# A three-layer transformer block on one core: first rows over two queues and two engines, gathers of first and second choices signalled apart, last results stored in halves, and a new order of all work

## The reference

```python
x = x + 0.5 * ffn(layernorm(x))
x = x + attn(layernorm(x))
x = x + 0.5 * ffn(layernorm(x))       # the same ffn and weights as in the first step
```

## Time and profile before

| | kernel before |
|---|---|
| median of 3 runs | 471.35 us (469.79 to 471.42) |
| profiled execution, whole | 470.26 us |
| span from its first to its last instruction | 468.5 us |
| mean granted TensorE clock | 0.993 of full speed |
| PE busy | 443.2 us, 95% of the span |
| PE weight loads (beside PE) | 377.1 us, 80% |
| DVE busy | 353.5 us, 75% |
| POOL busy | 281.6 us, 60% |
| ACT busy | 265.1 us, 57% |
| moved by DMA | 53.62 MB, 114 GB/s in the mean |

### The profile page before, as it was taken

The page is one execution under the profiler, slowest core; times in us unless marked ns, Lnnn a source line. Parts: engine busy times, 40 slices in busy tenths (PEclk is TensorE's granted clock), DMA queues, the critical chain, the costliest instruction groups (busy, mean ns, idle before and its releaser), DMA issues.

```text
span 468.5 us, 9695 instructions
## 1 busy us (share of the span) xinstructions
PE 443.2 (95%) x2959; PEld 377.1 (80%) x2959; DVE 353.5 (75%) x1112; ACT 265.1 (57%) x596; POOL 281.6 (60%) x290
## 2 busy tenths in 40 slices
PE   7999999999999999999899999998899999999992
PEld 3878878888889888879787788887779888887872
DVE  4899996333688978999899999998899743454553
ACT  5965145555766657667533675654285565565630
POOL 4127556777775067713878850777574767763771
PEclk9999999999999999999999999999899999999998
DMA  7991143355422334311113321221443445553332
GB/s 225 366 341 46 55 127 123 99 174 135 127 84 83 92 95 112 109 44 52 57 53 90 96 70 51 69 80 63 124 129 104 135 148 148 152 160 102 95 102 63
DMA packets 74210, 53.62 MB, mean 114 GB/s; under 512 B 9648, under 2 KB 68784, under 8 KB 74160
## 3 DMA queue, kind: packets, MB, share of 16 engines
q1 hardware_dynamic: 65968, 36.19, 26.1%
q0 software_dynamic: 8192, 16.79, 12.1%
HBM read 26.81 MB, written 26.15 MB: 113 GB/s over the span
## 4 chain that ended last, share of the span: by engine, by line
PE 49%; DVE 22%; POOL 12%; issue 8%; DMA 4%; ACT 3%; SPq 0%; POOLq 0%; DVEq 0%; ACTq 0%
PE pool L899 13%; POOL x_sorted L1150 6%; PE gu L847 6%; PE pool L888 6%; PE gu L849 6%; PE gu L848 6%; POOL yg L1170 4%; PE pool L830 3%; DVE X L1236 2%; DVE hs L1213 2%; DVE hs L1217 2%; DVE stats L1247 2%; PE gu L806 1%; ACT xn L1059 1%; DVE xt_lo L1269 1%
## 5 line engine op out<-in xcount | busy, mean ns | idle before, releaser
L1150 POOL DMA_INDIRECT x_sorted<-xn,places x128 | 130.0, 1016 | 64.1 <-issue 33.0
L1170 POOL DMA_INDIRECT yg<-y_sorted,places x128 | 123.7, 966 | 54.2 <-issue 35.7
L1036 ACT ACTIVATE gs<-gu 128x512 f32<-128x512 f32 x124 | 72.4, 584 | 74.3 <-PE gu L849 37.6
L1213 DVE TENSOR_TENSOR hs<-gs,gu 128x512 f32<-128x512 f32 x92 | 60.6, 663 | 59.3 <-ACT gs L1036 58.4
L899 PE MATMUL pool<-w,hT 128*128 x708 | 96.9, 281 | 0.1
L899 PEld LDWEIGHTS pool<-w,hT 128*128 128x128 f32 x708 | 87.4, 191 | 11.3 <-issue 7.7
L847 PE MATMUL gu<-w,xbt_hi 128*128 x177 | 82.4, 465 | 1.5 <-DVE hs L1217 0.9
L849 PE MATMUL gu<-w,xbt_hi 128*128 x177 | 70.3, 397 | 0.0
L848 PE MATMUL gu<-w,xbt_lo 128*128 x177 | 70.2, 396 | 0.0
L1042 ACT ACTIVATE hT<-pool 128x512 f32<-128x512 f32 x92 | 53.3, 581 | 24.0 <-PE pool L888 22.7
L1017 ACT ACTIVATE ys<-pool 128x256 f32<-128x256 f32 x92 | 34.5, 375 | 46.8 <-PE pool L899 46.5
(11 more groups left out here) (137 smaller groups left out, 765.4 us busy)
## 6 DMA issues: line engine op xcount, KB each, us to landing
xb<-x_sorted SPq DMA_DIRECT2D x85, 128.0 KB, 2.4
y_sorted<-ys SPq DMA_DIRECT2D x85, 128.0 KB
x_sorted<-yg SPq DMA_DIRECT2D x6, 512.0 KB, 7.7
X<-x_dram SPq DMA_DIRECT2D x8, 256.0 KB, 4.6
x_sorted<-xn,places POOLq DMA_INDIRECT x128, 2.3
yg<-y_sorted,places POOLq DMA_INDIRECT x128, 2.7
out_dram<-X SPq DMA_DIRECT2D x8, 256.0 KB
raw<-gate_w_dram SPq DMA_DIRECT2D x4, 256.0 KB, 4.9
```

Of the source, the lines that this page charges most:

```text
L1036: nc.scalar.activation(dst, src, ACT.Silu).then_inc(silu_done, 1)
L1150: nc.gpsimd.indirect_dma_start(x_sorted[g], bass.IndirectOffsetOnAxis(places[g][:, k, t:t + 1], 0), xn[:, b, t % T], None).then_inc(scatte ...
L1170: nc.gpsimd.indirect_dma_start(yg[slot][:, k, t], None, y_sorted[g], bass.IndirectOffsetOnAxis(places[g][:, k, at:at + 1], 0)).then_inc(ga ...
L1213: v.tensor_tensor(hs[n % HB][:].rearrange("p (j i) -> p j i", j=2)[:, 0:k], gs[n % GB][:].rearrange("p (j i) -> p j i", j=2)[:, 0:k], bank ...
```

## The change

**First rows.** The first sample's load is cut into two of 128 KB: tiles 0 and 1 on SP's queue, tiles 2 and 3 on ACT's, with a semaphore of their own. ACT also issues the loads of the shared gate and up weights; the shared down weights stay on SP and get a semaphore of their own, which `sdown` waits for. For (1, 0) alone, ACT normalizes tiles 0 and 1 and DVE tiles 2 and 3 (`norm_rest`); the transposes of tiles 2 and 3, and the scatters of that sample, wait for the latter.

**Gathers.** Each sample has one semaphore for its four gathers of first choices and one for its four of second choices. `add ... first` waits for the former, `add ... second` for the latter.

**Last results.** The last of the three adds of (3, b) raises `updated[b]` twice, after its first two tiles and after its last two (where the shared add is the last it is cut into two instructions); whoever needs the whole sample waits for 8 in place of 7 (`through`). SP stores each half with a transfer of 128 KB.

**Products.** `front` now waits for the high part before its first product and for the low part only before the third; for the experts and for keys and values the product with the low part of the moving rows becomes the third.

**Order.** `URGENCY` is a new string, and the lengths in `Plan` are changed: 71 for half of a `front` with 4 more until its result is seen, 179 for `sdown`, 104, 120 and 150 for `probs`, `best` and `second`, 120 for `root`, half the length of `pair_turn`, `hidden_turn` and `down` for a pair of a single block, and so on. The planned first add needs only the first four gathers, a scatter needs the `turn` of its sample, and a store of results takes 94 in place of 47.

```diff
-            load_x(0)
+            sp.dma_start(X[:, 0, 0:2], x[0].rearrange("(t p) d -> p t d", p=P)[:, 0:2]).then_inc(x_loaded[0], 16)
...
+            act.dma_start(X[:, 0, 2:4], x[0].rearrange("(t p) d -> p t d", p=P)[:, 2:4]).then_inc(x_rest_loaded, 16)
+            act.dma_start(raw[:, E, 0:I], sgate).then_inc(shared_loaded, 16)
+            act.dma_start(raw[:, E, I:GU], sup).then_inc(shared_loaded, 16)
...
+            def norm_rest(l, b):
+                once.wait_ge(shift_done[l], b + 1)
+                for t in (2, 3):
+                    ins = v.tensor_scalar(xn[:, b, t], X[:, b, t], rstd[:, l, b, t:t + 1], shifts[:, l, b, t:t + 1],
+                                          ALU.mult, ALU.add)
+                ins.then_inc(norm_rest_done, 1)
...
                 for t in range(T):
+                    if (l, b, t) == (1, 0, 2):
+                        once.wait_ge(norm_rest_done, 1)
                     mm = pe.transpose(pool_ps[m][:, t * P:(t + 1) * P], xn[:, b, t], ident)
...
-                    bass.IndirectOffsetOnAxis(places[g][:, k, at:at + 1], 0)).then_inc(gathered[b], 16)
+                    bass.IndirectOffsetOnAxis(places[g][:, k, at:at + 1], 0)).then_inc(gathered[b][k], 16)
...
-                if k == 0:
-                    once.wait_ge(gathered[b], 16 * 2 * T * (1 if l == 1 else 2))
-                    once.wait_ge(weigh_link, 3 * (g + 1))
+                once.wait_ge(gathered[b][k], 16 * T * (1 if l == 1 else 2))
+                once.wait_ge(weigh_link, 3 * (g + 1))
...
-                ins.then_inc(updated[b], 1)
+                    if t == T - 1 or (t == 1 and update(l, b, step) == LAST):
+                        ins.then_inc(updated[b], 1)
...
             def store_out(b):
-                once.wait_ge(updated[b], 7)
-                sp.dma_start(out[b].rearrange("(t p) d -> p t d", p=P), X[:, b]).then_inc(stored, 16)
+                for h in range(2):
+                    once.wait_ge(updated[b], LAST + h)
+                    half = slice(2 * h, 2 * h + 2)
+                    sp.dma_start(out[b].rearrange("(t p) d -> p t d", p=P)[:, half], X[:, b, half]).then_inc(stored, 16)
...
-                    once.wait_ge(xbt_lo_done, r + 1)
+                    once.wait_ge(xbt_hi_done, r + 1)
...
-                    pe.matmul(dst[:, j], xbt_lo[r % 2][:, at], hi, start=False, stop=False)
-                    mm = pe.matmul(dst[:, j], xbt_hi[r % 2][:, at], lo, start=False, stop=True)
+                    pe.matmul(dst[:, j], xbt_hi[r % 2][:, at], lo, start=False, stop=False)
+                    once.wait_ge(xbt_lo_done, r + 1)
+                    mm = pe.matmul(dst[:, j], xbt_lo[r % 2][:, at], hi, start=False, stop=True)
```

More of the change, by code:

```diff
@@ L142, in describe @@
             self.shared(3, b)
-            op(("out", b), "SP", 47, *(("add", 3, b, s) for s in ("first", "second", "shared")))
+            op(("out", b), "SP", 94, *(("add", 3, b, s) for s in ("first", "second", "shared")))
         for g in range(NG):
@@ L153, in norm @@
         op(("moments", l, b), "DVE", 50, ("stats", l, b))
-        op(("root", l, b), "POOL", 107, ("moments", l, b))
+        op(("root", l, b), "POOL", 120, ("moments", l, b))
         op(("shift", l, b), "DVE", 9, ("root", l, b))
@@ L162, in norm @@
         op(("norm", l, b, 0), "ACT", 80, ("shift", l, b), *free)
-        op(("norm", l, b, 1), "ACT", 80, ("norm", l, b, 0))
-        op(("turn", l, b), "PE", 290 if (l, b) == (1, 0) else 45, ("norm", l, b, 1), ("squares",), lands=-245 * ((l, b) == (1, 0)))
+        if (l, b) == (1, 0):
+            op(("norm_rest", l, b), "DVE", 44, ("shift", l, b))
+        else:
+            op(("norm", l, b, 1), "ACT", 80, ("norm", l, b, 0))
+        normed = ("norm_rest", l, b) if (l, b) == (1, 0) else ("norm", l, b, 1)
+        op(("turn", l, b), "PE", 290 if (l, b) == (1, 0) else 44, ("norm", l, b, 0), normed, ("squares",),
+           lands=-245 * ((l, b) == (1, 0)))
         op(("hi", l, b), "ACT", 50, ("turn", l, b))
@@ L182, in unit @@
         if halves == 2:
-            self.op(("front", u, 1), "PE", 73, *needs)
+            self.op(("front", u, 1), "PE", 71, *needs, lands=4)
             needs = (("front", u, 1),)
-        self.op(("front", u, 0), "PE", 73, *needs)
+        self.op(("front", u, 0), "PE", 71, *needs, lands=4)
     def gated(self, u):
@@ L200, in route @@
         op(("inverse", g), "DVE", 47, ("clamp", g))
-        op(("probs", g), "DVE", 92, ("inverse", g), ("sigmoid", g))
-        op(("best", g), "DVE", 116, ("probs", g))
-        op(("second", g), "DVE", 142, ("best", g))
+        op(("probs", g), "DVE", 104, ("inverse", g), ("sigmoid", g))
+        op(("best", g), "DVE", 120, ("probs", g))
+        op(("second", g), "DVE", 150, ("best", g))
         op(("choose", g), "DVE", 13, ("second", g))
@@ L216, in route @@
         for n in range(2 * tiles(g)):
-            op(("scatter", g, n), "POOL", 126, ("place", g), *free, ("norm", *GROUPS[g][n // 2 // T], 1), lands=200)
+            op(("scatter", g, n), "POOL", 126, ("place", g), *free, ("turn", *GROUPS[g][n // 2 // T]), lands=200)
             free = (("scatter", g, n),)
@@ L226, in experts @@
                 done = [("gather", l, b, n)]
-            op(("add", l, b, "first"), "DVE", 106, ("gather", l, b, 2 * T - 1), ("weigh", g))
-            op(("add", l, b, "second"), "DVE", 106, ("add", l, b, "first"))
+            op(("add", l, b, "first"), "DVE", 106, ("gather", l, b, T - 1), ("weigh", g))
+            op(("add", l, b, "second"), "DVE", 106, ("add", l, b, "first"), ("gather", l, b, 2 * T - 1))
     def routed(self, r, g, n):
@@ L696, in update, with through @@
             return (0 if l == 1 else 4) + done.index(step) + 1
+        def through(l, b, step):
+            n = update(l, b, step)
+            return LAST + 1 if n == LAST else n
         def freed(n):
@@ L1060, in normalize @@
                                                scale=rstd[:, l, b, t:t + 1])
-                if part == 1:
+                if part == 1 or (l, b) == (1, 0):
                     ins.then_inc(xn_done[l], 1)
@@ L1163, in gather @@
                     if old:
-                        once.wait_ge(updated[old[1]], update(*old, "second"))
+                        once.wait_ge(updated[old[1]], through(*old, "second"))
                     elif slot == YG - 1:
```

134 lines of the change are left out of this document (74 added, 60 removed).

## The result

The changed kernel takes 504.36 us (504.16 to 508.45 in 4 runs), the kernel before 471.34 in runs on the same chip: a ratio of 1.073 [1.0671, 1.0788], 33 us slower. The forecast was 466.0, with a range of 459.5 to 473.5: wrong in direction, and far outside.

What follows compares the result with a forecast made beforehand. PE, busy 443.2 of 468.5 us, was the fullest engine, DVE almost as full. From 470.26, gains of 0.5, 1.15, 0.2, 0.3 and 2.8 (4.95) gave 465.3; half of 1.1 added, 465.9, rounded to 466.0; range 459.5 to 473.5.

Steps and rivals of the forecast that it cites:

- New order: All engines' lists: a quarter of PE's 11.5 us idle in two stages won, 2.8 us; bounds gain 12, loss 7.4.
- A hold on POOL: Rival: a scatter held 7.4 us for PE where the chain runs through POOL; 475.5, near 476; chance 0.09.
- First rows on two queues: Head: the halved first load lands 0.1 us sooner; at best 1.0 sooner, at worst perhaps 0.3 lost.
- Two engines: Head, first normalization: ACT's two instructions take 0.81 us, DVE's two 0.59; transposes start 0.8 earlier, at about 7.8.
- The head's gain of 0.5: Head: what reaches the end from earlier transposes and high-part copy, 0.5 us, with the 0.1 of the queue in it.
- The rival of the second engine that waits: Head: POOL's root and DVE's two new instructions exclude one another; transposes only 0.1 us earlier, 466.4; chance 0.05.
- Low part awaited later: Products of 92 pairs: the added wait costs 0; bounds 9 us of loss and 0.5 of gain.
- Gathers apart and halves: Tail: 1.15 us from four adds leaving the end, 0.2 from half-size last stores; middle: 0.3 from shorter gather waits.
- Signs named ahead: Checks: PE idle from 200 to 345 us below 9.0; 4.8 to 5.0 us from last add to end.
- only the ends move: Rival: the old order fits as well, so only 0.5 + 1.35 us are left; 469.2; chance 0.18.
- the order wins much: Rival: the order gets most of PE's 11.5 us idle, 8 us in place of 2.8; 460.5; chance 0.14.
- the gathers and the halves do nothing: Tail rival: the new order puts the first add behind the last landing anyway, 1.35 us less gain; 467.5; chance 0.05.

Runs made afterwards that it cites:

- rope product 74: The kernel before with one plan length, the second rope product on VectorE, changed from 75 to 74 hundredths of a microsecond: 488.11 us, ratio 1.0363.
- first choice 117: The kernel before with one plan length, the first choice on VectorE, changed from 116 to 117 hundredths of a microsecond: 506.04 us, ratio 1.0792.
- scatter held back: The kernel before with one added plan need: group 4's last scatter waits until eight gathers of group 3 are issued: 494.29 us, ratio 1.0503.
- scatter's letter: The changed kernel with one letter of URGENCY changed, that of scatter 23 of group 4: 496.91 us, ratio 1.0549 to the kernel before.
- letter of pair 30: The changed kernel with one URGENCY letter changed, that of the second product of pair 30, from Q to ): 467.58 us, ratio 0.9919 to the kernel before.
- searched anew (wrong output): The changed kernel with the same lengths and all edits, but newly searched ranks in place of letters; output error 0.065: 469.58 us, ratio 0.9986.
- the tail's edits alone: The kernel before, in its own order, with only first- and second-choice gathers signalled apart and last results stored in halves: 468.58 us, ratio 0.9967.

## Why the prediction was wrong

The cause, as the runs show it, is the new order, and a bad order is a small step away from a good one. The letters of `URGENCY` are shifts that go with a set of lengths. A list scheduler that takes the best of what is ready can turn around two steps when a length moves by 0.01 us, and everything behind them is planned anew with shifts that were meant for another course: 17 and 35 us in the two kernels that differ from before in one length. How common that is, `Plan` itself tells, without the chip: with each length written in it made 0.01 us longer or shorter in turn, the planned end of the kernel before stays within 1 us in 72 of 158 cases, comes more than 20 us later in 73, and never comes more than 0.1 us earlier. In the changed kernel it stays within 1 us in 125 of 160 cases and comes more than 5 us earlier in 10. The first is the picture of letters tuned to their lengths; the changed kernel doesn't show it. The end of the plan, which the kernel's own `schedule` gives, beside the time on the chip (us):

| kernel | end of the plan | measured | difference |
|---|---|---|---|
| before | 461.4 | 471.3 | 9.9 |
| before, rope product 74 | 481.7 | 488.1 | 6.4 |
| before, first choice 117 | 500.2 | 506.0 | 5.8 |
| before, scatter held back | 487.3 | 494.3 | 7.0 |
| changed | 482.1 | 504.4 | 22.3 |
| changed, scatter's letter | 474.5 | 496.9 | 22.4 |
| changed, letter of pair 30 | 448.8 | 467.6 | 18.8 |
| changed, searched anew (wrong output) | 456.1 | 469.6 | 13.5 |

That one letter, that of pair 30, shortens the changed kernel's plan by 33 us says again that its letters are not the best for its lengths. Whether they were found for other lengths, or the search for them ended too early, can't be seen from the kernel.

Point by point:

**New order** (predicted a gain of 2.8, bounds a gain of 12 and a loss of 7.4): the step that failed. The difference between the changed kernel and all its edits in the old order is 504.4 - 469.5 = 34.9 us of loss. The plan's end accounts for 20.7 us of the 33; the rest is that the changed kernel stands further above its plan, which is left open below. The lower bound was one hold on POOL, as long as the longest in the earlier trace rows; that was the wrong kind of bound. A hold is a wait on a list that stays as it is. A new order can put one step behind 16 others, and the bound for that was to be had from the same trace: 16 gathers at 1.25 us make 20 us, and all pairs of a group stand behind the last scatter. Even that falls short: the loss is 34.9, and eight gathers, 10 us, went with 24. I also argued from the average (PE 9.0 idle, DVE nearly full) to what another order might win, and did not ask what the plan itself says of its end, which the kernel works out before its launch: 482.1 against 461.4.

**A hold on POOL** (the rival on the other side, 475.5 to 476): right in the engine, wrong in its mechanism and size. The waits of POOL in the changed kernel (us, times, longest us):

```profile
POOL x_sorted L1177 <- DVE places L1419: 22.6, 2, 18.3
POOL x_sorted L1177 <- PE gu L864: 19.9, 9, 15.0
POOL x_sorted L1177 <- PE gu L894: 12.5, 3, 10.7
```

They are longer than in the earlier trace rows, as the rival said. But the kernel with the letter of pair 30 has a long hold on such a scatter as well and loses nothing by it (its waits between 160 and 260 us):

```profile
POOL x_sorted L1177 <- PE gu L879: 10.0, 1, 10.0
```

And the scatter that cost so much waited for nothing: its bracket says 0.20, issue.

**First rows on two queues** (0.1, bounds 1.0 and -0.3): the first statistics start at 3.20 and not at 3.54, 0.34 earlier. What I left out is the second sample. Timeline of DVE, before:

```profile
5.33 0.87 DVE L1247 BATCH_NORM_STATS2 stats<-X 128x6 f32<-128x128 f32 x4 [0.23 <-DMA X<-x_dram]
...
6.72 0.15 DVE L1261 SCALAR_TENSOR_TENSOR shifts<-mv,rstd 128x4 f32<-128x4 f32 x1
```

and the head of the changed kernel:

```profile
1.23 0.50 ACTq L1029 DMA_DIRECT2D raw<-sgate_dram  x1
...
3.20 0.87 DVE L1280 BATCH_NORM_STATS2 stats<-X 128x6 f32<-128x128 f32 x4 [3.20 <-DMA X<-x_dram]
...
6.48 0.87 DVE L1280 BATCH_NORM_STATS2 stats<-X 128x6 f32<-128x128 f32 x4 [0.44 <-DMA X<-x_dram]
...
7.88 0.15 DVE L1294 SCALAR_TENSOR_TENSOR shifts<-mv,rstd 128x4 f32<-128x4 f32 x1
8.05 1.01 POOL L1157 TENSOR_TENSOR rstd<-ve,minus_half 128x4 f32<-128x4 f32 x1 [2.16 <-DVE ve L1290]
8.06 0.88 ACT L1084 ACTIVATE xn<-X,shifts,rstd 128x128 f32<-128x128 f32 x2 [1.59 <-DVE shifts L1294]
8.07 0.60 DVE L1300 TENSOR_SCALAR xn<-X,rstd,shifts 128x128 f32<-128x128 f32 x2
...
9.00 0.65 PE L948 MATMUL pool<-squares_sb,xn 128*128 128x128 f32 x4 [2.23 <-ACT xn L1084]
```

The second sample's statistics wait for its rows until 6.48, 1.15 later than before, and in DVE's list they stand ahead of the first sample's shift. ACT's queue now issues the shared weights at 1.23 and 1.76, beside SP's loads. The Trainium skill, "DMA: Bandwidth & Descriptors", section "Issuing engines are not separate DMA queues", says that transfers from several issuers share the same 16 DMA engines. These rows agree with it: the second sample's load is issued at 2.23, where it was 2.26, and its rows are there 1.15 later. No run parts the weights from the halves, so which of the two delays the rows is open.

**Two engines** (0.81 for two instructions on ACT, 0.59 for two on DVE): the sizes nearly hold, 0.88 and 0.60, and PE starts 0.06 behind ACT's end. But the shift comes 1.16 later, so the transposes start at 9.00, not 7.8 (8.61 before), and ACT's high-part copy at 9.69, not by 9.0. The head's gain of 0.5 is not shown: its edits alone have the ratio 0.9998 [0.998, 1.0016], an interval that would still hold a gain of 0.5, but their transposes start at 8.82, later than before. The rival of the second engine that waits is out by these rows: POOL's root (8.05, 1.01 long, as in the earlier trace rows) and DVE's two ran side by side, and neither took longer.

**Low part awaited later** (0, bound 9 of loss): right. All edits in the old order, with a wait more in each of 92 pairs, are 0.2% faster than before, where 9 us would be 1.9% slower. As the tail's edits alone gain 0.3%, about 0.5 us could be left for the waits, less than these runs tell apart. In a pair of the changed kernel the starts show no gap ahead of the third product either:

```profile
102.16 0.48 PE L861 MATMUL gu<-w,xbt_hi 128*128 x1
102.48 0.40 PE L862 MATMUL gu<-w,xbt_hi 128*128 x1
102.71 0.39 PE L864 MATMUL gu<-w,xbt_lo 128*128 x1
```

**Gathers apart and halves** (1.15, 0.3 and 0.2, 1.65 in all): the total is right. Alone in the old order they gain 0.33% [0.15, 0.5], 1.6 us of 470. The way is only partly the one I told. With the old list DVE takes the first add behind the last shared add, in the tail's edits alone:

```profile
459.84 0.76 DVE L1237 SCALAR_TENSOR_TENSOR X<-pool,X 128x256 f32<-128x256 f32 x2 [1.17 <-PE pool L919]
460.51 2.37 DVE L1247 SCALAR_TENSOR_TENSOR X<-yg,wsel,X 128x128 f32<-128x128 f32 x8
```

so all eight adds are still at the end, only 0.66 earlier than in the earlier trace rows, since the first four need not wait for the last landing. Where the rest of the 1.6 comes from, no row parts. Four adds alone behind the landing appear where the order was planned for it, in the changed kernel (494.50) and in the one with the letter of pair 30:

```profile
455.54 1.13 DVE L1266 SCALAR_TENSOR_TENSOR X<-yg,wsel,X 128x128 f32<-128x128 f32 x4
...
459.62 0.75 DVE L1256 SCALAR_TENSOR_TENSOR X<-pool,X 128x256 f32<-128x256 f32 x2 [1.10 <-PE pool L930]
460.29 1.13 DVE L1266 SCALAR_TENSOR_TENSOR X<-yg,wsel,X 128x128 f32<-128x128 f32 x4
```

There PE is late next: the shared add ends at 460.37 and the four adds follow it without a wait.

**Signs named ahead.** PE's idle time from 200 to 345 us was named as the sign for the order ("if it is the same or more, that step was wrong"): 15.9 against 9.0 told it at once. From the last add to the end I expected 4.8 to 5.0; it is 502.4 - 495.6 = 6.8.

**The rivals' sums.** By the prediction's own terms "only the ends move" comes to 469.0 (not 469.2), "the order wins much" to 460.8 (not 460.5) and "the gathers and the halves do nothing" to 467.4 (not 467.5). Nothing hangs on these tenths.

**Open.** The kernel with the letter of pair 30 ends 18.8 us above its plan, the old lengths' orders 6 to 10. The new lengths of PE's steps add up to 422.0 us, the old ones to 438.2, and PE was busy for 442.5 us in the kernel with the letter of pair 30 and for 443.2 in the kernel before. So the new lengths promise some 16 us that PE doesn't give, and the gain over before, 0.8%, is smaller than the plan's 12.6 us. That these lengths cause the gap is argued and was not tried.

## What to carry to other kernels

An order that was searched for exact lengths is part of the tuning of those lengths: change one, even by 0.01 us, and the planned end has to be looked at, and the list searched again where it has grown, before anything else is credited or blamed. Judge an edit in the old order first; here the edits together are worth 0.2%, and the kernels with other orders lie between 0.8% below and 7.9% above the kernel before. For a new order, do not bound the loss by the longest wait of the old trace. Ask for the longest run of steps that can come to stand ahead of one on which a whole group hangs, and expect more than its length: here the losses that went with such a run were about twice as long.

## What the runs showed of the hardware

PE's granted clock fell to 0.56 over 15 us, in the middle of the kernel, after PE had been idle for 3.9 of the 15 us before; PE's busy time grew by 5.6 us for the same 2959 products. An order with holes is thus paid for a second time.

At the end, SP waits for PE's sequencer 4.7 us in the changed kernel and 2.6 before (us, times, longest us); first after, then before:

```profile
SPq L542 <- PEq L542: 4.7, 1, 4.7
```
```profile
SPq L535 <- PEq L535: 2.6, 1, 2.6
```

It was 3.2 with all edits in the old order, 4.2 with the letter of pair 30, and 1.1 in the kernel before with 117 for the first choice. The 2.1 us of difference between after and before are more than the 1.8 by which the end lies further behind the last add; what sets this wait, no run tells.
